# Wide attention as one pipeline over the batches of both stages, with 64-row products side by side and three PSUM banks taking turns

## The reference

```python
def cross_attention(x, ctx, wq, wk, wv, wo, bo):
    q = jnp.einsum('bne,ef->bnf', x, wq)      # 320 -> 1280, 20 heads of 64
    k = jnp.einsum('bme,ef->bmf', ctx, wk)    # 320 or 192 -> 1280
    v = jnp.einsum('bme,ef->bmf', ctx, wv)
    attn = jax.nn.softmax(q @ k.T * SCALE, axis=-1)   # per head, 512 x 512
    return (attn @ v) @ wo + bo
x = cross_attention(ln(x), ln(x), ...) + x    # stage s0
x = cross_attention(ln(x), context, ...) + x  # stage s1
x = geglu_ff(ln(x), ...) + x                  # stage s2
```

## Time and profile before

| | us |
|---|---|
| median of 3 runs (lowest, highest) | 4240.84 (4230.23, 4243.2) |
| profiled execution, its own time | 4228.71 |
| span in the profile | 4226.6 |
| PE busy, share of the span | 3774.3, 89% |
| DVE, ACT, POOL busy | 1754.6, 1538.5, 677.8 |
| wide stages s0 and s1, from the start to the last residual | 1932.3 |
| feed-forward s2; s5 | 300.6; 301.2 |
| narrow stages s3 and s4; s7 | 868.9; 465.4 |
| gated stage s6 | 357.6 |

### The profile page before, as it was taken

How to read it: one execution, slowest core, us unless ns; L and a number is a source line. 1 busy time by engine, 2 the same in 40 slices (tenths; PEclk the granted TensorE clock), 3 DMA queues, 4 the chain that set the end, 5 groups by cost and what they waited for, 6 DMA issues and landing times.

```text
span 4226.6 us, 39174 instructions
## 1 busy us (share of the span) xinstructions
PE 3774.3 (89%) x15784; PEld 1553.7 (37%) x15784; DVE 1754.6 (42%) x2338; ACT 1538.5 (36%) x2113; POOL 677.8 (16%) x438
## 2 busy tenths in 40 slices
PE   8999899998989899998996898999889978868997
PEld 3333333333333333334442333333334455542332
DVE  2524335252534435352123665666611222225553
ACT  3424243342524344341111554555521111114553
POOL 1414223141423324240000000000000000000000
PEclk9999999999979989999996999999999976758998
DMA  2000000001000000001000000000010010000000
GB/s 80 16 15 23 12 23 4 27 12 46 16 14 22 11 19 7 26 10 49 0 1 19 1 1 16 4 12 1 1 49 0 0 31 8 4 23 4 5 1 25
DMA packets 43235, 67.35 MB, mean 16 GB/s; under 512 B 5296, under 2 KB 30320, under 8 KB 43056
## 3 DMA queue, kind: packets, MB, share of 16 engines
q1 hardware_dynamic: 43056, 64.85, 5.1%
HBM read 62.22 MB, written 2.62 MB: 15 GB/s over the span
## 4 chain that ended last, share of the span: by engine, by line
PE 79%; DVE 11%; ACT 3%; issue 3%; DMA 2%; SPq 1%; POOL 0%; DVEq 0%; ACTq 0%; POOLq 0%
PE bank L498 11%; PE bank L576 7%; PE bank L431 7%; PE bank L465 6%; PE bank L922 5%; PE bank L551 5%; DVE heads L879 4%; PE bank L864 4%; PE bank L1411 4%; PE bank L847 4%; PE bank L1413 3%; PE bank L1039 3%; DVE negm L528 3%; PE bank L520 2%; PE bank L975 2%
## 5 line engine op out<-in xcount | busy, mean ns | idle before, releaser
L879 DVE TENSOR_REDUCE heads<-bank 128x2 f32<-128x1024 f32 x480 | 587.8, 1225 | 513.9 <-PE bank L864 511.6
L528 DVE TENSOR_REDUCE negm<-bank 128x2 f32<-128x1024 f32 x320 | 387.9, 1212 | 954.5 <-PE bank L520 954.5
L431 PE MATMUL bank<-weights,mixed 128*128 128x320 f32 (+1 forms) x1376 | 398.0, 448 | 19.8 <-DVE mixed L1440 12.6
L551 PE MATMUL bank<-weights 64*128 64x512 f32 x1280 | 411.7, 628 | 0.0
L498 PE MATMUL bank<-hT,heads 128*128 128x512 f32 x720 | 382.6, 653 | 16.1 <-issue 8.9
L431 PEld LDWEIGHTS bank<-weights,mixed 128*128 128x128 f32 (+1 forms) x1376 | 261.7, 194 | 160.1 <-issue 32.8
L610 DVE RECIPROCAL rec<-ox 128x128 f32<-128x128 f32 x320 | 279.0, 918 | 94.2 <-ACT ox L615 88.5
L847 PE MATMUL bank<-heads 32*128 32x512 f32 x1920 | 312.2, 634 | 5.9 <-ACT weights L892 3.0
L892 ACT ACTIVATE weights<-bank 128x1024 f32<-128x1024 f32 x238 | 230.6, 1021 | 104.7 <-PE bank L847 104.5
L864 PE MATMUL bank<-heads 32*128 32x512 bf16 x960 | 194.0, 401 | 65.8 <-DVE heads L879 57.2
L587 POOL TENSOR_TENSOR heads<-probs 128x1024 f32<-128x1024 f32 x40 | 95.8, 2394 | 838.0 <-ACT probs L566 838.0
(11 more groups left out here) (172 smaller groups left out, 5162.6 us busy)
## 6 DMA issues: line engine op xcount, KB each, us to landing
heads<-in_wqk SPq DMA_DIRECT2D x40, 384.0 KB, 3.0
heads<-in_wqk SPq DMA_DIRECT2D x40, 320.0 KB, 2.9
ctx_in<-in_ctx SPq DMA_DIRECT2D x16, 384.0 KB, 3.5
weights<-in_L_xattn_wo SPq DMA_DIRECT2D x2, 1600.0 KB, 13.8
x_res<-in_x SPq DMA_DIRECT2D x4, 640.0 KB, 12.8
out<-x_res SPq DMA_DIRECT2D x1, 2560.0 KB, 8.7
weights<-in_L_xattn_w_ff SPq DMA_DIRECT2D x1, 1600.0 KB, 13.0
weights<-in_L_xattn_ff_w SPq DMA_DIRECT2D x1, 1600.0 KB, 12.0
```

What stands on the lines that cost most here:

```text
L431: last = nc.tensor.matmul(M.SM[t % 2][:, 0:D], v["OT"][0:w, c, t * P:t * P + P], v["wo"][0:w, c, :], start=c == 0, stop=c == nch - 1)
L528: nc.vector.tensor_reduce(M.negm[:, u % 2, i, 0:2], M.ROWS[:, :, :], AX.X, ALU.max, negate=True).then_inc(s.sem("max"), 1)
L551: nc.tensor.matmul(out[:, g, :], v["KT"][strip, u % 3, i * P:i * P + P], v["QT"][strip, u % 3, :], start=True, stop=False)
L879: nc.vector.tensor_reduce(v["negm"][:, tile, qb, 64 * half:64 * half + 64].rearrange("p (g k) -> p g k", g=2)[:, :, at], M.ROWS4[:, :, :], ...
```

## The change

The two wide stages become one run over 8 batches (`WideRun`). A batch `n` has 40 steps `i`, four for each pair of heads; a step is one block of scores, the rows product of 5 steps later, and the product with the values of the step before. The inputs, projections and values of batch `n + 1` and the output product of batch `n - 1` sit in given steps of batch `n`. All of these, with the maxima and sums, take one of three banks (`WX`) in turn. The scores have one pair of banks, the probabilities one buffer, the attention outputs 13 slots in place of 10.

The 64-row chunks of q and k are computed first, q's from partitions 0 to 63 and k's from 64 to 127, into two banks (`w_QK_first`); likewise those of the first two value slices (`w_V_first`). The host packs the weights for it. The weights of s1 go to places of their own and are loaded ahead.

In the feed-forward the inputs of the next batch come ahead of the output product, and its norm after block 4 of 10. In the narrow runs `negm_pe4` and `negm_dve4` move behind the rest of their step, ACT's input copies wait for three small loads alone, and those of s4 are loaded ahead. The gated stage keeps its work.

```diff
-        self.COLS = [self.pair[2], self.pair[0]]
+        self.COLS = self.pair[0]
+        self.WOB = self.pair[2][:, 0, :]
+        self.WX = [self.pair[2][:, 1, :]] + self.bank[6:8]
...
+                v["probs"] = M.probs[:, :, :, :].rearrange("p a (b g) n -> p (a b) g n", g=2)
...
+                v["OT"] = [M.mixed[:, c * N:c * N + N] for c in range(10)] + [M.heads[:, 8448 + c * N:8448 + c * N + N] for c in range(3)]
...
+                items = []
+                now, new, old = 0 <= n < self.N, n + 1 < self.N, 0 <= n - 1
+                if kb == 3 and (new if u == 9 else now):
+                    items += [(f"negm{(u + 1) % 10}", n + 1 if u == 9 else n)]
+                if kb == 0 and (now if u < 8 else new):
+                    w, m = ((u + 2) % 10, n if u < 8 else n + 1)
+                    items += [(f"Q{w}", m), (f"K{w}", m)]
+                if i in (33, 35, 37, 39) and new:
+                    items += [("V0_%d" % ((i - 33) // 2), n + 1), ("V1_%d" % ((i - 33) // 2), n + 1)]
+                if i in (17, 21, 23, 25) and now:
+                    items += [("V2_%d" % (17, 21, 23, 25).index(i), n)]
+                if i in (7, 9, 11, 13) and old:
+                    items += [("y%d" % ((i - 7) // 2), n - 1)]
+                if i == 29 and new:
+                    items += [("T0", n + 1), ("T1", n + 1)]
+                if i == 30 and new:
+                    items += [("T2", n + 1)] + ([("C0", n + 1)] if self.cross[n + 1] else [])
+                if i == 31 and new and self.cross[n + 1]:
+                    items += [("C1", n + 1)]
+                if kb == 2 and (old if u == 0 else now):
+                    items += [(f"den{(u - 1) % 10}", n - 1 if u == 0 else n)]
...
+        def w_scores(pe, r, n, i):
+
+            v, u, kb, U = n_view(r, n), i // 4, i % 4, 10 * n + i // 4
+            r.wait(pe, "exp", 40 * n + i)
+            for g in range(2):
+                strip = slice(64 * g, 64 * g + 64)
+                nc.tensor.matmul(M.COLS[:, g, :], v["KT"][strip, U % 3, kb * P:kb * P + P], v["QT"][strip, U % 3, :], start=True, stop=False)
+            if kb == 0:
+                r.wait_out(pe, f"negm{u}", n)
+            for g in range(2):
+                strip = slice(64 * g, 64 * g + 64)
+                last = nc.tensor.matmul(M.COLS[:, g, :], M.sel[strip, :], M.nmT[strip, U % 2, :], start=False, stop=True)
+            last.then_inc(r.sem("cols"), 1)
...
+        def w_rows_pe(pe, r, n, i):
+            at = w_ahead(r, n, i)
+            if at is None:
+                return
+            n, u, qb = at
+            v, U = n_view(r, n), 10 * n + u
+            if qb == 0:
+                r.wait_out(pe, f"Q{u}", n)
+                r.wait_out(pe, f"K{u}", n)
+            r.wait(pe, "max", 4 * U + qb)
+            for g in range(2):
+                strip = slice(64 * g, 64 * g + 64)
+                last = nc.tensor.matmul(M.ROWS[:, g, :], v["QB"][strip, U % 2, qb * P:qb * P + P], v["KB"][strip, U % 2, :], start=True, stop=True)
+            last.then_inc(r.sem("rows"), 1)
...
+        def w_exp_act(act, r, n, i):
+
+            v, kb, U = n_view(r, n), i % 4, 10 * n + i // 4
+            r.wait(act, "mix", 40 * n + i - 3)
+            r.wait(act, "part", 3 * (U - 1) + (1, 1, 2, 3)[kb])
+            r.wait(act, "cols", 40 * n + i + 1)
+            nc.scalar.activation(v["probs"][:, kb, :, :], M.COLS[:, :, :], ACT.Exp, scale=float(r.work[n][0].prm["dh"]) ** -0.5).then_inc(r.sem("exp"), 1)
...
+        def w_sum_pool(pool, r, n, u):
+
+            v, U = n_view(r, n), 10 * n + u
+            pr, ps = v["probs"], v["psum"][:, U % 2, :, :]
+            if U >= 2:
+                r.wait_full(pool, f"den{(U - 2) % 10}", (U - 2) // 10)
+            r.wait(pool, "exp", 4 * U + 2)
...
+        def w_mix_pe(pe, r, n, i):
...
+                return
+            v, u, kb, U = n_view(r, n), i // 4, i % 4, 10 * n + i // 4
+            if u == 0:
+                r.wait_out(pe, f"V1_{kb}", n)
+            if u == 8:
+                r.wait_out(pe, f"V2_{kb}", n)
+            if kb == 0:
+                r.wait(pe, "ob", U)
+            r.wait(pe, "exp", 40 * n + i + 1)
+            for g in range(2):
+                last = nc.tensor.matmul(M.WOB[64 * g:64 * g + 64, :], v["V"][:, kb, 2 * u + g, :], v["probs"][:, kb, g, :], start=kb == 0, stop=kb == TB - 1)
+            last.then_inc(r.sem("mix"), 1)
...
+        def w_den_pe(pe, r, n, u):
+            v, item, U = n_view(r, n), f"den{u}", 10 * n + u
+            r.wait_free(pe, item, n)
+            r.wait(pe, "part", 3 * U + 3)
+            for g in range(2):
+                last = nc.tensor.matmul(r.bank_of(item, n)[64 * g:64 * g + 64, :], M.ones[:, :], v["psum"][:, U % 2, g, :], start=True, stop=True)
+            last.then_inc(r.full(item, n), 1)
...
+        def w_QK_first(pe, r, n, u):
+
...
+            q, k, w, kT = r.bank_of(f"Q{u}", n), r.bank_of(f"K{u}", n), v["wqk"][U % 2], kvT(s)
+            r.wait(pe, f"wqk{U % 2}", 16 * (U // 2 + 1))
+            if u == 0:
+                r.wait_out(pe, "T2", n)
+                r.wait_out(pe, "C1", n)
+            r.wait_free(pe, f"Q{u}", n)
+            r.wait_free(pe, f"K{u}", n)
+            nc.tensor.matmul(q[:, :], w[0:64, 2, :], M.hT[0:64, 2, :], start=True, stop=False)
+            nc.tensor.matmul(k[:, :], w[64:P, 2, :], kT[64:P, last_chunk(s), :], start=True, stop=False)
+
+        def w_QK_rest(pe, r, n, u):
+            s, v, U = r.work[n][0], n_view(r, n), 10 * n + u
+            q, k, w, kT, last_k = r.bank_of(f"Q{u}", n), r.bank_of(f"K{u}", n), v["wqk"][U % 2], kvT(s), last_chunk(s)
+            for e in range(2):
+                last = nc.tensor.matmul(q[:, :], w[:, e, :], M.hT[:, e, :], start=False, stop=e == 1)
+            last.then_inc(r.full(f"Q{u}", n), 1)
+            for e in range(last_k):
+                last = nc.tensor.matmul(k[:, :], w[:, 3 + e, :], kT[:, e, :], start=False, stop=e == last_k - 1)
+            last.then_inc(r.full(f"K{u}", n), 1)
...
+        def w_QK_act(act, r, n, u, which):
+            v, item, U = n_view(r, n), f"{which}{u}", 10 * n + u
+            r.wait_full(act, item, n)
+            r.wait(act, "cols", 4 * (U - 2))
+            r.wait(act, "rows", 4 * (U - 1))
+            nc.scalar.copy(v[which + "T"][:, U % 3, :], r.bank_of(item, n)[:, :])
+            nc.scalar.copy(v[which + "B"][:, U % 2, :], r.bank_of(item, n)[:, :]).then_inc(r.free(item, n), 1)
...
+        def w_V_first(pe, r, n, t):
+
+            s, v = r.work[n][0], n_view(r, n)
+            kT, tt, wv, c = kvT(s), slice(t * P, t * P + P), v["wv"], last_chunk(s)
+            banks = [r.bank_of(f"V{j}_{t}", n) for j in range(2)]
+            pe.wait_ge(s.sem("wv_in" + s.tag), 48)
+            if t == 0:
+                r.wait_out(pe, "T2", n)
+                r.wait_out(pe, "C1", n)
+            for j in range(2):
+                r.wait_free(pe, f"V{j}_{t}", n)
+            for j in range(2):
+                strip = slice(64 * j, 64 * j + 64)
+                nc.tensor.matmul(banks[j][:, :], kT[strip, c, tt], wv[strip, c, 512 * j:512 * j + 512], start=True, stop=False)
...
+        def wide_pe(pe, r):
+            for n in range(-1, r.N + 1):
+                now, new, old = 0 <= n < r.N, n + 1 < r.N, 0 <= n - 1
+                for i in range(40):
+                    u, kb = i // 4, i % 4
+                    if now:
+                        w_scores(pe, r, n, i)
+                    w_rows_pe(pe, r, n, i)
+                    if kb == 3 and u < 9 and now:
+                        w_negm_pe(pe, r, n, u + 1)
+                    if kb == 3 and u == 9 and new:
+                        w_negm_pe(pe, r, n + 1, 0)
+                    if kb == 0 and u < 8 and now:
+                        w_QK_first(pe, r, n, u + 2)
+                    if kb == 0 and u >= 8 and new:
+                        w_QK_first(pe, r, n + 1, u - 8)
+                    if i in (33, 35, 37, 39) and new:
+                        w_V_first(pe, r, n + 1, (i - 33) // 2)
+                    if i in (17, 21, 23, 25) and now:
+                        w_V2_first(pe, r, n, (17, 21, 23, 25).index(i))
+                    w_mix_pe(pe, r, n, i)
+                    if kb == 0 and u < 8 and now:
+                        w_QK_rest(pe, r, n, u + 2)
+                    if kb == 0 and u >= 8 and new:
+                        w_QK_rest(pe, r, n + 1, u - 8)
+                    if i in (33, 35, 37, 39) and new:
+                        w_V_rest(pe, r, n + 1, (i - 33) // 2)
+                    if i in (17, 21, 23, 25) and now:
+                        w_V2_rest(pe, r, n, (17, 21, 23, 25).index(i))
+                    if i in (7, 9, 11, 13) and old:
+                        w_y_pe(pe, r, n - 1, (i - 7) // 2)
+                    if i == 29 and new:
+                        w_T_pe(pe, r, n + 1, 0)
+                        w_T_pe(pe, r, n + 1, 1)
+                    if i == 30 and new:
```

(29 more changed lines are left out.)

763 lines of the change are left out of this document (375 added, 388 removed).

## The result

The changed kernel takes 3836.3 us in the median of 4 runs (3819.49 to 3841.67), the kernel before beside it 4235.53; the ratio is 0.9074, 95% interval 0.9045 to 0.9103. The prediction said 3876 (3800 to 3985). The profiled execution took 3841.67 us, its span is 3839.9, 386.7 less than the span before.

A forecast was written before the change was run, and what follows sets the result against it. PE was taken to set the pace in the wide stages, busy 1795.3 of 1932.3 us. Savings of 276 (wide), 12 (feed-forward), 60 (s3, s4) and 17 (s7) sum to 365: 4240.8 - 365 = 3876 us, range 3800 to 3985.

The forecast's parts named there:

- Wide, the work: Wide stages: pairs 1228 us, values 180, output product 173, transposes 22, together 1603 us of PE work.
- A pair saves 1.0 us: Wide pairs: side-by-side 64-row chunks save 1.28 us, three more changes of matmul kind cost 0.27.
- the whole overhang: Tiling-mode drain taken as a rows product's full overhang: three more changes would cost 38 us over 80 pairs, not 22.
- Wide, the idle time: Wide stages: one start and end replace eight; two batches' worth of idle time and lost clock stay, 53 us.
- Wide, the dependencies costed at nothing: Wide pipeline: scores waiting for the previous step's exponential, with one pair of banks, cost nothing; called the weak step.
- the rival of waits in the pairs: Wide pairs: PE waits for ACT once a pair by k's two copies, 94 us, so 3970; chance 0.19.
- The slower rival: Wide steps: every exponential wholly uncovered, 358 us over 320 steps, 4234 or over 4250 with lower clock; chance 0.03.
- The 64-row chunks: Wide q, k and values: two 64-row chunks run side by side in 1.06 us, as in the feed-forward.
- Feed-forward: Feed-forward: inputs ahead of the output product save 2 us at six batch changes, 12 us; about 1 us waiting stays each.
- The term of 60 us: s3 and s4: 18 us at transposes, 8 rows cover, 11.9 bank, 10.8 weights, 3 at start, some 8 clock.
- The second rows product gets the transposes as cover for its reduce; I take 8: s3 and s4: moved transposes cover the second rows product's reduce, taking 8 us off L864's 32.5 us wait.
- the narrow reordering costs: Narrow stages: maxima bank frees late, so the 60 and 17 us are lost and some 20 added, 3973; chance 0.05.

The follow-up runs named there:

- The cut pipeline: Changed kernel with the wide pipeline cut in two runs, one for s0 and one for s1: 3849.5 us, ratio 0.911.
- the old guard: DVE's earlier wait before a group's first reduce, for the previous group's transposes: 4267.83 us with only the moved transposes in the kernel before, 3927.59 in the changed kernel.

## Why the prediction was right

**Wide, the work.** I forecast 1603 us of work (the 22 for transposes should be 8 x 2 + 4 x 1.2 = 20.8, so 1602); the window has PE busy for 1603.1. A batch of s0 was 10 x 15.8 + 27.6 + 21.6 + 2 = 209.2 by my terms and measured 208.0, one of s1 191.4 and 191.9. The terms are not each as good: a pair without other work takes 15.98 (from one `L681` to the next), the values of a block 6.2 in s0 instead of 6.9, the output product 22.3 instead of 21.6. They cancel, and that the sum is right to 1 us is luck.

"A pair saves 1.0 us" was too much: it is 17.05 - 0.24 - 15.98 = 0.83. q and k now take 4.59 us, a little under the forecast, but they took less than 5.94 before, since k's 64-row product ran beside the scores: from 866.35 to 870.61 in that timeline there are k's projection and a step's scores, maxima and rows, 4.26 us together, of which the latter are 1.49 by 866.35 - 864.86, so 2.77 is left for k instead of 2.97. The values product in four pieces of a pair takes 3.98 us where it took 3.64 in two, 0.34 more, where I had 0.27 for three changes. So a change costs about 0.09 around the values products but 0.15 at the 64-row products put apart, which is the size of the whole overhang (0.16) that I had set aside. The pair's 15.98 lies nearer to that figure (16.0) than to my 15.8, though q and k are the larger part of the difference.

**Wide, the idle time.** This term was mis-sized, and it holds nearly all of the 30 us that the wide stages gained beyond the forecast. I left 34 us of idle time and 19 of clock; measured are 22.9, of them 11.1 at the very start for the first norm, and a clock of 1.00 in the window, so next to nothing. I had priced start and end by two batches of the old kernel, 27 us each. The cut pipeline puts one start with one end at 19 us in the new form. The old average was no price for a start and an end anyway, since not all of the 137 us were that. From PE's waits in the wide stages of the kernel before:

```profile
PE bank L534 <- DVE negm L528: 40.6, 16, 2.5
PE bank L520 <- DVE negm L528: 22.2, 88, 0.3
PE bank L379 <- DMA ctx_in<-in_ctx: 19.7, 4, 11.9
```

The second line lies inside the pairs: I took it out of the pair as 0.24 us and left it in the 137. The third is contexts, one of them for 11.9 us. All three are gone. No run has the new wide pipeline in the kernel before with all else left as it was: its 306.3 us are read from the traces, as 114 us less idle time and 192 less busy time, and the runs here price only the joint and the placing of the 64-row products.

**Wide, the dependencies costed at nothing.** Right, and now with a size: in 2 of 40 steps nothing is left, in the others 0.55 us or more. What the rival of waits in the pairs would take can be read from that: even two more copies of ACT in every step cost 54 us and not its 94. The Trainium skill, TensorEngine Tiling, PSUM Bottleneck, spoke for this rival; with 0.9 us of waits the trace does not show the emptying of PSUM as a limit here. The slower rival, each exponential uncovered, is far off.

**The 64-row chunks.** They run side by side, and fully: 0.95 us for both. The 1.06 that I took from the earlier trace rows stands behind a full product, as the 1.05 of k's product alone does, so it holds a change that I counted again.

**Feed-forward.** Mechanism right, 15.0 instead of 12. The 1 us left at each change of batch is there. The rest comes in part from the starts of s2 and s5, whose waits I had left out: they are some 2 us shorter each (3.2 + 3.9 us in s2 before, 1.9 + 2.8 now).

**Narrow.** The term of 60 us was 16 too high, and one step failed. "The second rows product gets the transposes as cover for its reduce; I take 8": measured 33.8 us after 32.5, nothing, with the rows products that had a reduce to wait for waiting as before. The 18 for the transposes came as 23.1 - 6.3 = 16.8, since ACT's copy ahead of the output product, whose bank the transposes take, is late in 6 of 40 places. The bank's 11.9, the 10.8 of s4's weights, 2.2 at the start and 6.6 us less busy time match their terms of 12, 11, 3 and 8. In s7 it is 24 instead of 17: 14.4 of idle time and 9.6 of busy time at the better clock, which I had left out.

**What the prediction did not see.** It costed the moved transposes without asking who waits for them on DVE. With the old guard the move loses 48 us in the kernel before and 97 us against the changed kernel; that is the prediction's rival "the narrow reordering costs", with another mechanism than the bank it named. That this part came out as it did is luck as far as the prediction goes: the changed line saved it, and the reasoning did not cover that line.

## What to carry to other kernels

When an instruction is moved on one engine, list every wait on the other engines that names its semaphore, the guards of buffers above all: a guard that names a later event than it must is free as long as that event is early, and here turned a gain of 1.4% into a loss of 1.1%. When double buffers are given up for a pipeline, measure the slack step by step as the time from the end of the one engine's work to the start of the next on the other; from it the price of any further work can be read, in start-to-start times and not in shown durations. Joining batches saves the fill and the drain once per joint (19 us here, by the cut pipeline). At the edges of stages that stay, look next for loads that wait although their memory is free earlier.

## What the hardware showed that was not expected

Two products of 64 rows in the two halves of the rows took 0.95 us, the same as one alone (0.94): the second is free, not merely cheap. In 1626 us of nearly gapless work PE's granted clock stood at 1.00, with 0.96 before; s6, which waits in short pieces throughout, was granted 0.66, and 17 us less idle time there brought 24 us of busy time back, while at the start of s3 21 us less brought under 3. A change of tiling had no single price: about 0.09 us around the values products, 0.15 around the 64-row products put apart.
